# Scores of several attention heads in one PSUM bank: one mask matmul and one maximum per bank, orders rearranged

## The reference

```python
x = x + 0.5 * ffn(layernorm(x))    # 16 experts, F = 96, the best 2 per token, silu(g) * u
x = x + attn(layernorm(x))         # 16 heads of 128, 4 key/value heads, rotary, causal softmax
x = x + 0.5 * ffn(layernorm(x))    # the same weights as in the first step
# in attn, for each batch and head:
scores = (q @ k.T) * 128 ** -0.5 + causal_add      # causal_add: -2.4e38 above the diagonal
out = softmax(scores) @ v                          # then @ Wo
```

## Time and profile before

| | |
|---|---|
| median of 3 runs | 896.63 us |
| the 3 runs | 894.85, 896.63, 899.28 us |
| span of the profiled execution | 899.0 us |
| PE busy | 805.2 us, 90% of the span |
| DVE, ACT, POOL busy | 646.9, 573.7, 454.5 us |
| mean granted TensorE clock | 0.975 |

### The profile page before, as it was taken

One profiled execution on the slowest core, in us unless ns is written; L12 is line 12 of the kernel. 1 busy time (PEld: TensorE's weight loads), 2 busy tenths in 40 slices (PEclk: granted clock), 3 DMA queues, 4 the chain that ended last, 5 costly groups with the idle time before them and its releaser, 6 DMA issues.

```text
span 899.0 us, 16806 instructions
## 1 busy us (share of the span) xinstructions
PE 805.2 (90%) x4840; PEld 680.3 (76%) x4840; DVE 646.9 (72%) x1580; ACT 573.7 (64%) x1538; POOL 454.5 (51%) x410
## 2 busy tenths in 40 slices
PE   3788899799999999999999999999889879899990
PEld 3677678578878888887888887888777668787870
DVE  5855565478887777887978878877579957756573
ACT  3355556677776877776777777677566655555550
POOL 1473504487465775664656655445243684003274
PEclk9999989999999999999999999999899999999995
DMA  9398953211000100010000000000000055257685
GB/s 295 115 292 262 281 143 100 74 16 24 1 1 14 18 14 7 1 17 9 1 13 12 1 1 1 1 2 2 7 1 1 25 201 157 70 150 205 192 245 175
DMA packets 52952, 70.73 MB, mean 79 GB/s; under 512 B 7552, under 2 KB 44672, under 8 KB 52480
## 3 DMA queue, kind: packets, MB, share of 16 engines
q1 hardware_dynamic: 40768, 47.61, 17.2%
q0 software_dynamic: 9216, 16.82, 7.6%
q10 hardware_dynamic: 2880, 5.24, 2.0%
HBM read 42.61 MB, written 27.03 MB: 77 GB/s over the span
## 4 chain that ended last, share of the span: by engine, by line
PE 55%; issue 13%; POOL 13%; DVE 9%; ACT 4%; DMA 3%; POOLq 0%; ACTq 0%; DVEq 0%; SPq 0%
PE ps L1648 45%; PE ps L1846 5%; POOL xs L1558 3%; POOL xs L1565 3%; POOL sb_ropeB L1593 2%; POOL sb_xf L1596 2%; PE ps L1702 2%; POOL sb_x L1584 2%; DVE sb_x L1444 1%; PE ps L1665 1%; POOL sb_wF L1604 1%; POOL sb_wF_raw L1579 1%; PE ps L1716 1%; DVE sb_wF L1424 1%; ACT sb_prob L985 1%
## 5 line engine op out<-in xcount | busy, mean ns | idle before, releaser
L1648 PE MATMUL ps<-sb_wF 128*128 128x512 f32 (+2 forms) x1056 | 280.3, 387 | 15.6 <-DVE sb_wF L1434 5.8
L1648 PEld LDWEIGHTS ps<-sb_wF 128*128 128x128 f32 x1056 | 170.6, 192 | 29.7 <-DVE sb_wF L1424 8.7
L1593 POOL TENSOR_TENSOR sb_ropeB<-sb_ropeB,sb_sin 128x512 f32<-128x512 f32 x80 | 107.7, 1346 | 147.8 <-ACT sb_ropeB L965 147.3
L985 ACT ACTIVATE sb_prob<-ps,sb_nmax 128x128 f32<-128x128 f32 (+3 forms) x256 | 134.4, 526 | 62.9 <-DVE sb_nmax L1417 61.6
L1648 PE MATMUL ps<-sb_wF,sb_wA 128*128 128x512 f32 x576 | 156.0, 406 | 5.9 <-ACT sb_ropeB L965 4.4
L1417 DVE TENSOR_REDUCE sb_nmax<-ps 128x1 f32<-128x128 f32 (+3 forms) x256 | 121.4, 482 | 49.5 <-PE ps L1648 47.7
L1424 DVE TENSOR_TENSOR sb_wF<-ps,sb_wF 128x512 fp32r<-128x512 f32 x160 | 109.2, 683 | 39.2 <-ACT sb_wF L994 38.8
L1604 POOL TENSOR_TENSOR sb_wF<-sb_xf,sb_wF 128x384 fp32r<-128x384 f32 (+1 forms) x75 | 84.0, 1121 | 98.1 <-ACT sb_wF L977 98.0
L1444 DVE SCALAR_TENSOR_TENSOR sb_x<-ps,sb_rinv,sb_x 128x256 f32<-128x256 f32 x256 | 122.4, 478 | 15.6 <-PE ps L1648 6.6
L1648 PEld LDWEIGHTS ps<-sb_wF,sb_wA 128*128 128x128 f32 x576 | 103.2, 191 | 26.8 <-ACT sb_ropeB L965 5.6
L1648 PE MATMUL ps<-sb_wA,sb_wF 128*128 128x256 f32 x768 | 115.6, 287 | 4.1 <-DVE sb_x L1444 2.1
(11 more groups left out here) (203 smaller groups left out, 1322.4 us busy)
## 6 DMA issues: line engine op xcount, KB each, us to landing
ys<-sb_wA_raw SPq DMA_DIRECT2D x124, 128.0 KB, 2.5
sb_wF_raw<-xs SPq DMA_DIRECT2D x44, 128.5 KB, 4.5
sb_wA_raw<-xs SPq DMA_DIRECT2D x44, 128.5 KB, 2.6
sb_work<-xs SPq DMA_DIRECT2D x36, 128.5 KB, 2.7
sb_wA_raw<-in_wattn ACTq DMA_DIRECT2D x18, 256.0 KB, 4.7
sb_wF_raw<-in_wgu SPq DMA_DIRECT2D x4, 768.0 KB, 10.9
sb_wF_raw<-in_wdn SPq DMA_DIRECT2D x4, 768.0 KB, 12.4
sb_wA_raw<-in_wgu SPq DMA_DIRECT2D x4, 768.0 KB, 8.0
```

The source lines that it names most:

```text
L985: nc.scalar.activation(prob[k % 2][:, h, 0:(i + 1) * P], ps[:, bank_of((k * G + h) % (UB * G)), 0:(i + 1) * P], ACT.Exp, bias=nmax[:, k % ...
L1593: nc.gpsimd.tensor_tensor(ropeB[:, slot], ropeB[:, slot], sin[:], ALU.mult).then_inc(rope_mul, 1)
L1648: return nc.tensor.matmul(out, lhsT, rhs, start=start, stop=stop)
```

## The change

- The 4 heads of query tile 0 share one bank (4 x 128 columns), the heads of tile 1 two and two (2 x 256 columns); tiles 2 and 3 keep a bank for each head. A group has 11 score steps in place of 16. Banks 0 to 2 are still taken in turn, now by step, and a step waits for the last exponential that read the step three before.
- In a bank start is set on the first head's first matmul alone. One mask matmul ends the bank: all its heads at once (the mask is repeated by a stride of 0, and the output goes to each head's diagonal block). Its weights are 127 columns of `identb`, for all tiles: the last query of a tile has nothing to mask.
- One maximum is taken for each bank, with one result for each head. The exponentials stay one for each head.
- The order lists drop the steps that are gone. S,0,0 (all four heads) stands at the start of the group; S,1,0 moves ahead of V,-1,1 and S,1,2 ahead of J,0,0; max,1,2 stands where max,1,1 was. ACT's and POOL's lists are unchanged. The ahead-of-time list `BESIDE` and one key of `AFTER` follow.

```diff
-    def bank_of(m):
-        return SBANK + (1 if m == UB * G - 1 else m % 3)
+    def score_parts(b, k):
+        shared = {0: G, 1: G // 2}.get(tile_of(*own_unit(b, k)), 1)
+        return [range(h, h + shared) for h in range(0, G, shared)]
+    def own_unit(b, k):
+        return b + k // UB, k % UB
+    SPG = 1 + 2 + 2 * G
+    def score_step(b, k, h):
+        b, k = own_unit(b, k)
+        g, u = divmod(k, T)
+        before = sum(len(score_parts(b, g * T + v)) for v in range(u))
+        return (b * KV + g) * SPG + before + next(n for n, hs in enumerate(score_parts(b, k)) if h in hs)
+    def score_bank(step):
+        return SBANK + step % 3
+    def scores_at(b, k, h):
+        i = tile_of(*own_unit(b, k))
+        hs = next(hs for hs in score_parts(b, k) if h in hs)
+        at = (h - hs[0]) * (i + 1) * P
+        return ps[:, score_bank(score_step(b, k, h)), at:at + (i + 1) * P]
...
+                LAST_READ[score_step(b_, k_, h_)] = b_ * UB * G + k_ * G + h_ + 1
...
         "pe": """
-        S,0,0 S,0,1 T,-1,0 V,-2,2 W,-3,1 T,-1,1 J,0,4 S,0,2 V,-1,0 T,-1,2 S,0,3 V,-1,1 W,-2,0 T,-1,3 S,1,0 S,1,1
-        V,-1,2 J,0,0 W,-2,1 V,-1,3 T,0,0 S,1,2 S,1,3 S,2,0 J,0,1 W,-1,0 V,0,0 T,1,0 S,2,1 S,2,2 W,-1,1 J,0,2
+        S,0,0 T,-1,0 V,-2,2 W,-3,1 T,-1,1 J,0,4 V,-1,0 T,-1,2 S,1,0 V,-1,1 W,-2,0 T,-1,3
+        V,-1,2 S,1,2 J,0,0 W,-2,1 V,-1,3 T,0,0 S,2,0 J,0,1 W,-1,0 V,0,0 T,1,0 S,2,1 S,2,2 W,-1,1 J,0,2
...
         "dve": """
-        pt_lo,-2,2 x_add2,-3,0 max,0,0 recip,-1,0 max,0,1 pt_lo,-1,0 x_add,-3,1 a_lo,-2,0 x_add2,-3,1 pt_lo,-1,1
-        Jd,0,4 max,0,2 max,0,3 pt_lo,-1,2 x_add,-2,0 max,1,0 x_add2,-2,0 pt_lo,-1,3 recip,0,0 max,1,1 Jd,0,0
-        x_add,-2,1 x_add2,-2,1 max,1,2 a_lo,-1,0 pt_lo,0,0 max,1,3 max,2,0 Jd,0,1 x_add,-1,0 recip,1,0
+        pt_lo,-2,2 x_add2,-3,0 max,0,0 recip,-1,0 pt_lo,-1,0 x_add,-3,1 a_lo,-2,0 x_add2,-3,1 pt_lo,-1,1
+        Jd,0,4 pt_lo,-1,2 max,1,0 x_add,-2,0 x_add2,-2,0 pt_lo,-1,3 recip,0,0 max,1,2 Jd,0,0
+        x_add,-2,1 x_add2,-2,1 a_lo,-1,0 pt_lo,0,0 max,2,0 Jd,0,1 x_add,-1,0 recip,1,0
...
         def maximum(b, k, h):
-            nc.vector.tensor_reduce(nmax[:, k % 2, h:h + 1], ps[:, bank_of((k * G + h) % (UB * G)), 0:(i + 1) * P],
+            nc.vector.tensor_reduce(nmax[:, k % 2, heads[0]:heads[-1] + 1],
+                                    ps[:, score_bank(step), 0:width].rearrange("p (h c) -> p h c", h=len(heads)),
                                     AX_X, ALU.max, negate=True).then_inc(nmax_done, 1)
...
         def scores_of(b, k, h):
-            if not (b == 0 and m < 3):
-                pe.wait_ge(exp_done, b * UB * G + m - bank_before(m) + 1)
+            if step >= 3:
+                pe.wait_ge(exp_done, LAST_READ[step - 3])
...
+            for n in heads:
+                if u < 2:
+                    pe.wait_ge(q_hi if i == 0 else q_lo, (G + 1) * (KV * b + g) + 2 + n)
+                o = scores_at(b, k, n)
+                if i == 0:
+                    mm(o, first_q(g, n), first_k(g), n == heads[0], False)
+                else:
+                    mm(o, q_at(g, n, 0)[:, rows], k_at(g, 0)[:, 0:(i + 1) * P], n == heads[0], False)
+                    mm(o, q_at(g, n, 0)[:, rows], k_at(g, 1)[:, 0:(i + 1) * P], False, False)
+                    mm(o, q_at(g, n, 1)[:, rows], k_at(g, 0)[:, 0:(i + 1) * P], False, False)
-            mm(o[:, rows], identb[:], causal[:], False, True).then_inc(s_done, 1)
+            whole = ps[:, score_bank(step), 0:len(heads) * (i + 1) * P].rearrange("p (h c) -> p h c", h=len(heads))
+            mask = causal[:].rearrange("p (o c) -> p o c", o=1).broadcast_to([P, len(heads), P])
+            mm(whole[0:P - 1, :, rows], identb[:, 0:P - 1], mask, False, True).then_inc(s_done, 1)
```

More of the change, by code:

```diff
@@ L257, in tiles_before @@
         return g * T * (T + 1) // 2 + sum(tile_of(b, g * T + u) + 1 for u in range(i))
-    def bank_of(m):
-        return SBANK + (1 if m == UB * G - 1 else m % 3)
-    def bank_before(m):
-        M = UB * G
-        return next(d for d in range(1, 9) if bank_of((m - d) % M) == bank_of(m % M))
+    def score_parts(b, k):
[16 more added lines that the diff above has]
+        return ps[:, score_bank(score_step(b, k, h)), at:at + (i + 1) * P]
     KCOL, VCOL, VALUES = G, G + 1, G + 2
@@ L268, in program @@
     LN_GROUP = KV - 2
+    LAST_READ = {}
+    for b_ in range(B):
+        for k_ in range(UB):
+            for h_ in range(G):
+                LAST_READ[score_step(b_, k_, h_)] = b_ * UB * G + k_ * G + h_ + 1
     ORDER = {
         "pe": """
-        S,0,0 S,0,1 T,-1,0 V,-2,2 W,-3,1 T,-1,1 J,0,4 S,0,2 V,-1,0 T,-1,2 S,0,3 V,-1,1 W,-2,0 T,-1,3 S,1,0 S,1,1
-        V,-1,2 J,0,0 W,-2,1 V,-1,3 T,0,0 S,1,2 S,1,3 S,2,0 J,0,1 W,-1,0 V,0,0 T,1,0 S,2,1 S,2,2 W,-1,1 J,0,2
+        S,0,0 T,-1,0 V,-2,2 W,-3,1 T,-1,1 J,0,4 V,-1,0 T,-1,2 S,1,0 V,-1,1 W,-2,0 T,-1,3
+        V,-1,2 S,1,2 J,0,0 W,-2,1 V,-1,3 T,0,0 S,2,0 J,0,1 W,-1,0 V,0,0 T,1,0 S,2,1 S,2,2 W,-1,1 J,0,2
         T,1,1 S,2,3 V,1,0 W,0,0 S,3,0 J,0,3 W,0,1 T,2,0 V,1,1 S,3,1 J,0,5 T,2,1 S,3,2 V,2,0 J,0,6 S,3,3 T,2,2
@@ L307, in program @@
         x_add2,-2,1 max,1,1 a_lo,-1,0 pt_lo,0,1 max,1,2 x_add,-1,0 x_add2,-1,0 pt_lo,0,2 max,1,3 x_add,-1,1
-        max,2,0 x_add2,-1,1 recip,1,0 a_lo,0,0 pt_lo,1,0 max,2,1 pt_lo,1,1 max,2,2 x_add,0,0 x_add2,0,0 max,2,3
-        pt_lo,1,2 x_add,0,1 max,3,0 x_add2,0,1 recip,2,0 pt_lo,1,3 max,3,1 pt_lo,2,0 a_lo,1,0 max,3,2 pt_lo,2,1
-        max,3,3 x_add,1,0 x_add2,1,0 recip,3,0 pt_lo,3,0 a_lo,2,0 x_add,1,1 x_add2,1,1 x_add,2,0 x_add2,2,0
+        max,2,0 x_add2,-1,1 recip,1,0 a_lo,0,0 pt_lo,1,0 max,2,2 pt_lo,1,1 x_add,0,0 x_add2,0,0 max,3,0
+        pt_lo,1,2 x_add,0,1 x_add2,0,1 recip,2,0 pt_lo,1,3 pt_lo,2,0 a_lo,1,0 pt_lo,2,1
+        x_add,1,0 x_add2,1,0 recip,3,0 pt_lo,3,0 a_lo,2,0 x_add,1,1 x_add2,1,1 x_add,2,0 x_add2,2,0
         a_lo,3,0 x_add,2,1 x_add2,2,1""",
@@ L564, in program @@
     W_LANDED = 16 * (GU_PARTS + DN_PARTS)
-    BESIDE = {"pe": {-1: [("S", 0, 0), ("S", 0, 1)], 0: [("J", 0, 4)]}, "dve": {0: [("max", 0, 0), ("max", 0, 1)]}}
+    BESIDE = {"pe": {-1: [("S", 0, 0)], 0: [("J", 0, 4)]}, "dve": {0: [("max", 0, 0)]}}
     def head_of(engine):
@@ L971, in rope_hi @@
             if k >= 0:
-                act.wait_ge(s_done, b * UB * G + max((g - 1) * T * G, 1))
+                act.wait_ge(s_done, b * KV * SPG + max((g - 1) * SPG, 1))
             whole = xf[:, rope_slot(col)]
@@ L1411, in maximum @@
         def maximum(b, k, h):
-            i = tile_of(b, k)
-            m = b * UB * G + k * G + h
-            dve.wait_ge(s_done, m + 1)
+            step = score_step(b, k, h)
+            heads = next(hs for hs in score_parts(b, k) if h in hs)
+            dve.wait_ge(s_done, step + 1)
             if not (b == 0 and k < 2):
-                dve.wait_ge(exp_done, m - 2 * G + 1)
-            nc.vector.tensor_reduce(nmax[:, k % 2, h:h + 1], ps[:, bank_of((k * G + h) % (UB * G)), 0:(i + 1) * P],
+                dve.wait_ge(exp_done, b * UB * G + (k - 2) * G + heads[-1] + 1)
+            width = len(heads) * (tile_of(*own_unit(b, k)) + 1) * P
+            nc.vector.tensor_reduce(nmax[:, k % 2, heads[0]:heads[-1] + 1],
+                                    ps[:, score_bank(step), 0:width].rearrange("p (h c) -> p h c", h=len(heads)),
                                     AX_X, ALU.max, negate=True).then_inc(nmax_done, 1)
```

25 lines of the change are left out of this document (8 added, 17 removed), and 2 rows, old and new, of the table AFTER.

## The result

The changed kernel takes **905.63 us** (median of 4 runs, 903.68 to 908.31) beside 895.74 us for the kernel before on the same chip (4 runs, 891.89 to 899.28): a ratio of 1.011, 95% interval 1.0081 to 1.014. Forecast were 890.7 us, faster by 0.7%; it is slower by 1.1%. The profiled execution has a span of 901.6 us. Of the 9.9 us between the medians the traces show 5.4 against that second execution and 2.6 against the first: the changed kernel's profiled run is the fastest of its four, and before's two lie above its median.

The account below looks back on a forecast made before the run. PE was taken to bound the attention up to about 690 us. Ten groups at 0.48 gave 4.8, plus 1.0 for other groups and 1.0 for bank waits, less 0.9: 896.6 - 5.9 = 890.7 us, range 885 to 897.5.

Parts of the forecast that it names:

- The price of the masks: PE's mask matmuls in an unhindered group: 0.48 us saved (0.25 to 1.00), from tiles 0, 1 and 2 to 3.
- Rival 2: Masks of tiles 2 and 3: the 127-column load is not hidden, +8.8 us, 905.4; chance 0.09.
- S,0,0 with all four queries, max,0,0: Group start: scores needing all four rotated queries have 1.0 us of cover, and the longer maximum is covered; no cost.
- The thin place J,0,1: PE's J,0,1 behind DVE's product: cover falls from 1.2 to 0.2 us; 0.9 lost in three groups, bound 3.0.
- the six others: First two and last four groups: four counted at half the saving, 1.0 us gained, the last two at nothing.
- Bank waits, 1.0 gained: S,1,0 no longer waits for its own group's exponentials; 0.30 to 0.33 us idle in three groups, 1.0 gained.
- Rival 1: Cover at J,0,1 gone in all ten groups, 3.0 us, and bank waits become DVE waits; 893.8, chance 0.22.
- Rival 3: The load behind the mask hides too, masks fall to stream, 0.5 us more a group; 884.7, chance 0.08.
- Rival 4: Nothing gained: a group is held by DVE's order and not by PE; 896.6, chance 0.06.

Follow-up runs that it names:

- that second execution: The kernel before, unchanged, profiled a second time as a control; span 896.2 us, measured 897.3 us, ratio 1.0005.
- e1: The kernel before with 127 weight columns in each of its 256 masks; 895.3 us, ratio 0.9984.
- e2: The changed kernel with all 128 columns in the masks again; 905.3 us, ratio 1.0101.
- e3: The changed kernel with S,1,2 put back behind T,0,0 on PE and max,1,2 behind x_add2,-2,1 on DVE; 900.2 us, ratio 1.0031.
- e9: The changed kernel with five empty places in VectorE's list where maxima were removed, so steps placed by share keep their old neighbours; 903.6 us, ratio 1.0068.
- e14: The kernel before with 127-column masks, and norm steps and products behind J,0,6 at the changed kernel's places; 891.3 us, ratio 0.9948.
- e11: The kernel before with the second feed-forward part's routing steps at the places they have in the changed kernel; 900.5 us, ratio 1.004.

## Why the prediction was wrong

- **The price of the masks: right.** 0.48 a group was forecast, 0.47 to 0.49 came in the groups that PE fills, and 0.01 a mask for 127 columns (e1, e2). Rival 2 is out: the longer load of 127 columns hides (0.136 us, no idle time ahead of it). Its 905.4 is nearly the measured time by coincidence; the masks got cheaper, and other things cost.
- **S,0,0 with all four queries, max,0,0: right.** Neither shows as a wait in groups 4 to 7.
- **The thin place J,0,1: right place, wrong size.** 0.9 was forecast, 3.0 the bound. Measured, from start to start: 0.99 in groups 6 and 10 and 4.1 in group 14, 6.1 in all (the 4.1 stands in place of a wait of 2.3 at V, and is counted among the six others below too), and in group 13 the later J,0,3 and J,0,5 wait 1.2 and 1.3. The step counted the product's own time and 0.7 us of norm statistics. It did not read VectorE's list around Jd,0,0 in each group: a norm step that POOL stretches from 0.16 to 1.30, and the routing block. In group 5, where I did have rows, the place held. There W waits instead (0.54 in the changed kernel, 0.30 in e3), behind another norm step that POOL stretches.
- **Bank waits, 1.0 gained: wrong.** The wait on an exponential did go, and what was late next took its place: e9 has the looser banks and 38.1 in group 7, e14 the old banks and 36.0. The gain there is that of the slid norm steps and products, 2.1 us in each of two groups (1.7 from e1 to e14).
- **"The six others" at half and nothing: this step failed most.** Groups 12 to 14 lost 6.8 us against the second execution of before and 2.4 against the first, where 1.0 had been put down as gained in four of the six. I took their waits as given, and masks as all that the change brings there. Two things were missed. The edit shortens a list in which other steps are placed by share; that costs 3.0 to 4.6 us (e9, e11). And waits there are paid twice where the clock falls behind them: groups 12 to 14 ran 17 us at 1.2 GHz, in place of 7 and 10 in the two executions before; over all timed runs the mean granted clock is 0.969 (4 runs) beside 0.976 (29 runs).
- **Rival 1** named the mechanism, waits that eat the gain, at 3.0 us; its price is what was wrong. Rival 3 is out. Rival 4 is out for the full groups, which got shorter; VectorE's order did decide in the others, at a price that rival 4 put at nothing.

Open stays why the clock falls behind the wait at 634 in some executions of one kernel and not in others. Open stays too where the rest of the 9.9 us lies that no pair of traces shows (4.5 against the second execution), and what causes the 0.8 us that group 0 lost and the 1.1 of group 2; in group 2 W's wait ends at 256.9 in both kernels, so what PE saved ahead of it is given back.
